# Adding the identity to W's blocks, starting the sums with ScalarE's copies, and building the images without rows of the first layer

## What is computed

```python
B_req = B[adapter_ids]; A_req = A[adapter_ids]
Bx = jnp.einsum('bni,bri->bnr', x, B_req)
out = jnp.einsum('bnr,bor->bno', Bx, A_req)            # layer 0, SCALING 1
...
base_out = jnp.einsum('bti,oi->bto', x, W) + b
lora_h = jnp.einsum('bti,bir->btr', x, A)
lora_out = jnp.einsum('btr,bro->bto', lora_h, Bm)
return base_out + lora_out * SCALING                   # layer 1, SCALING 2
...
x = x + _L0_cond_ref(x, L0_cond_A, L0_cond_B, itok_B_4_50)
x = x + _L1_cond_ref(x, itok_B_0_23, L1_cond_W, L1_cond_b, L1_cond_lora_As, L1_cond_lora_Bs)
```

## Time and profile before

| | before |
|---|---|
| median of 3 runs | 1411.78 us (1410.3 to 1412.83) |
| profiled execution | 1409.31 us |
| its span, first to last instruction | 1407.5 us |
| PE busy | 1373.3 us (98%) |
| DVE busy | 967.0 us (69%) |
| ACT busy | 484.7 us (34%) |
| POOL busy | 94.1 us (7%) |
| bytes moved | 320.98 MB, 228 GB/s over the span |
| granted TensorE clock, mean | 0.994 |

### The profile page before, as it was taken

The page is one execution under the profiler, slowest core; times in us unless marked ns, Lnnn a source line. Parts: engine busy times, 40 slices in busy tenths (PEclk is TensorE's granted clock), DMA queues, the critical chain, the costliest instruction groups (busy, mean ns, idle before and its releaser), DMA issues.

```text
span 1407.5 us, 16133 instructions
## 1 busy us (share of the span) xinstructions
PE 1373.3 (98%) x5992; PEld 1128.7 (80%) x5992; DVE 967.0 (69%) x1015; ACT 484.7 (34%) x491; POOL 94.1 (7%) x194
## 2 busy tenths in 40 slices
PE   5999989999999999999999999999999999999999
PEld 4787778888878888888888888888888888888887
DVE  5778777786768897666646676666655766666662
ACT  3444344323223333333323343333233334332331
POOL 3013210001000000000001000000101000000000
PEclk9999999999999999999999999999999999999999
DMA  9988863798999898466757334456856444457642
GB/s 348 317 291 292 282 233 131 258 376 300 317 355 336 302 303 291 166 220 233 240 198 241 128 120 156 169 187 214 276 199 228 141 137 135 154 171 249 197 152 83
DMA packets 106094, 320.98 MB, mean 228 GB/s; under 512 B 14240, under 2 KB 15392, under 8 KB 106016
## 3 DMA queue, kind: packets, MB, share of 16 engines
q1 hardware_dynamic: 99360, 307.35, 63.8%
q0 software_dynamic: 6656, 12.60, 2.8%
HBM read 264.31 MB, written 55.57 MB: 227 GB/s over the span
## 4 chain that ended last, share of the span: by engine, by line
PE 86%; DMA 6%; DVE 4%; issue 2%; SPq 1%; ACT 1%; POOLq 0%; POOL 0%; DVEq 0%; ACTq 0%
PE acc L546 26%; PE acc L547 26%; PE acc L548 26%; PE down_ps L516 2%; PE acc L530 2%; PE down_ps L517 2%; DMA bg_raw<-w_rows 1%; DMA w_two<-w 1%; DVE bg_lo L720 1%; DMA w_sums<-w_one 1%; DVE w_one L689 1%; DVE w_lo L693 1%; DMA bg_raw<-x 1%; PE image_ps L498 1%; DMA image<-a 1%
## 5 line engine op out<-in xcount | busy, mean ns | idle before, releaser
L546 PE MATMUL acc<-x_hi,w_hi 128*128 128x512 f32 x1792 | 704.5, 393 | 18.9 <-DVE x_lo L715 13.6
L547 PE MATMUL acc<-x_lo,w_hi 128*128 128x512 f32 x1792 | 701.4, 391 | 0.0
L548 PE MATMUL acc<-x_hi,w_lo 128*128 128x512 f32 x1792 | 700.9, 391 | 0.0
L583 ACT ACTIVATE w_hi<-w_one 128x1024 fp32r<-128x1024 f32 x224 | 237.4, 1060 | 679.1 <-PE acc L548 620.2
L546 PEld LDWEIGHTS acc<-x_hi,w_hi 128*128 128x128 f32 x1792 | 338.6, 189 | 92.8 <-issue 14.0
L547 PEld LDWEIGHTS acc<-x_lo,w_hi 128*128 128x128 f32 x1792 | 338.7, 189 | 71.8 <-issue 1.0
L548 PEld LDWEIGHTS acc<-x_hi,w_lo 128*128 128x128 f32 x1792 | 338.1, 189 | 71.4
L693 DVE TENSOR_TENSOR w_lo<-w_one,w_hi 128x1024 fp32r<-128x1024 f32 x224 | 273.7, 1222 | 110.1 <-ACT w_hi L583 110.1
L758 DVE SCALAR_TENSOR_TENSOR sums<-acc,bias_sb,sums 128x512 f32<-128x512 f32 x128 | 95.7, 748 | 43.6 <-PE acc L530 43.6
L715 DVE TENSOR_TENSOR x_lo<-x_stage,x_hi 128x1024 fp32r<-128x1024 f32 x80 | 96.1, 1222 | 43.0 <-ACT x_hi L602 42.8
L602 ACT ACTIVATE x_hi<-x_stage 128x1024 fp32r<-128x1024 f32 x80 | 83.4, 1056 | 103.9 <-DVE x_stage L709 82.2
(11 more groups left out here) (54 smaller groups left out, 628.6 us busy)
## 6 DMA issues: line engine op xcount, KB each, us to landing
w_one<-w SPq DMA_DIRECT2D x128, 512.0 KB, 5.6
w_one<-w_sums SPq DMA_DIRECT2D x96, 512.0 KB, 3.2
w_two<-w SPq DMA_DIRECT2D x64, 512.0 KB, 8.0
x_stage<-x SPq DMA_DIRECT2D x64, 512.0 KB, 4.6
out<-sums SPq DMA_DIRECT2D x128, 256.0 KB, 4.4
w_sums<-w_one SPq DMA_DIRECT2D x40, 512.0 KB, 5.3
resident<-x SPq DMA_DIRECT2D x32, 512.0 KB, 7.0
sums<-x SPq DMA_DIRECT2D x64, 256.0 KB, 4.9
```

Source lines behind the costliest of these rows:

```text
L546: pe.matmul(ps[:, :], w_hi[ws][:, c, :], hi, start=(c == 0), stop=False)
L547: pe.matmul(ps[:, :], w_hi[ws][:, c, :], lo, start=False, stop=False)
L548: mm = pe.matmul(ps[:, :], w_lo[ws][:, c, :], hi, start=False, stop=(c == H - 1))
L583: act.activation(w_hi[s % W_PARTS][:, :, :], w_one[s % W_ONES][:, :, :], ACT.Copy).then_inc(w_hi_ready, 1)
```

## The change

Instead of adding x when the banks are added, the identity (times -1, 1 or 2) is added to the diagonal part of W's blocks, so that the seven products give x (I + W^T). `make_w` does this in VectorE behind the sum, for 128 blocks. The tiles of `sums` now begin with ScalarE's copy of a bank (products 0, 1 and 4), VectorE's `add` has one addition where it had two in products 0 and 1, and none in product 4; `load_sum` is gone. Low-rank rows of layer 0 come into the image over TensorE (`wa` times the identity, 128 columns). The images' tile is now `b1_rows` itself; the closing product stands one step later at c = 6, and VectorE's copy one round later. Chunks of x (`z >= IMAGE`) are loaded a step earlier.

```diff
+W_IDENTITY = [-1.0, 2.0, 1.0, 1.0, -1.0, 1.0, 1.0]
+COPIED = [0, 1, 4]
...
-            image = sb("image", [P, T], F32, early)
...
+        image = b1_rows
...
             def keep_sum(s):
                 if keeps_sum(s):
-                    sp.wait_ge(w_summed, sums_before(s) + 1)
+                    sp.wait_ge(w_made, made_before(s) + 1)
...
                 for z in background(s + 2):
-                    load_bg(z)
-                if s + 2 < STEPS:
-                    load_sum(s + 2)
+                    if z < IMAGE:
+                        load_bg(z)
+                for z in background(s + 3):
+                    if z >= IMAGE:
+                        load_bg(z)
...
             def load_rows(j):
                 cols = slice(T * j, T * (j + 1))
                 if j:
-                    pool.wait_ge(image_done, j)
+                    keep_image(j - 1)
+                    pool.wait_ge(image_stored, DMA * j)
                 for n in range(NB):
                     pool.dma_start(b1_rows[R * n:R * (n + 1), :], adapter(1, n, b1).rearrange("u r d -> (u r) d")[:, cols])\
                         .then_inc(b1_rows_loaded, DMA)
-                if j:
-                    keep_image(j - 1)
-                    pool.wait_ge(image_stored, DMA * j)
-                for n in range(NB):
-                    pool.dma_start(image[R * n:R * (n + 1), :], adapter(0, n, a0).rearrange("u r d -> (u r) d")[:, cols])\
-                        .then_inc(a0_rows_loaded, DMA)
...
             pool.dma_start(ids_sb[:, 1, :], ids1).then_inc(ids_loaded, DMA)
+            pool.dma_start(identity_sb[:, :], identity).then_inc(identity_loaded, DMA)
...
+                        if c // BANKS == j:
+                            part = ps[:, P * (c % BANKS):P * (c % BANKS + 1)]
+                            pe.matmul(part, wa[0], identity_sb[:, :], start=False, stop=False)
+                            pe.matmul(part, wa[1], identity_sb[:, :], start=False, stop=False)
...
+            def end_image(j):
+                pe.wait_ge(across_ready, 1)
+                pe.wait_ge(b1_rows_loaded, NB * DMA * (j + 1))
+                pe.matmul(image_ps[j % 2][:, :], across[:, :], b1_rows[:, :],
+                          start=False, stop=True).then_inc(image_done, 1)
...
-                if i != 6:
-                    pe.wait_ge(first_added, 24 * g + 8 * (i - 3) + o + 1)
+                if i == 4:
+                    pe.wait_ge(copied, copied_before(s) + 1)
...
+                    if c == 6 and s - 1 in IMAGE_LAST:
+                        end_image(IMAGE_LAST[s - 1])
...
+            def copy(s):
...
+                if i == 1:
+                    act.wait_ge(bank_free, released_before(s) + 1)
+                else:
+                    act.wait_ge(step_done, s + 1)
...
+                act.activation(sums[1 if i == 1 else 2][:, o, :], acc[s % BANKS][:, :], ACT.Copy).then_inc(copied, 1)
...
+                    dve.wait_ge(w_summed, k + 1)
+                if s == 0:
+                    dve.wait_ge(identity_loaded, DMA)
+                dve.scalar_tensor_tensor(out=one[:, o, :], in0=f32(identity_sb[:, :]), scalar=W_IDENTITY[i],
+                                         in1=one[:, o, :], op0=ALU.mult, op1=ALU.add).then_inc(w_made, 1)
...
-                if s - 1 in IMAGE_LAST:
-                    j = IMAGE_LAST[s - 1]
+                if s - 2 in IMAGE_LAST:
+                    j = IMAGE_LAST[s - 2]
                     dve.wait_ge(image_done, j + 1)
-                    dve.wait_ge(a0_rows_loaded, NB * DMA * (j + 1))
-                    dve.tensor_tensor(image[:, :], image_ps[j % 2][:, :], image[:, :], ALU.add).then_inc(image_ready, 1)
+                    dve.tensor_copy(image[:, :], image_ps[j % 2][:, :]).then_inc(image_ready, 1)
```

More of the change, by code:

```diff
@@ L129, in has_sum, with is_made, made_before, copied_before @@
     return s >= 0 and i in SUMMED and g <= KEPT_IN[i]
+def is_made(s):
+    return s >= 0 and (has_sum(s) or where(s)[1] not in SUMMED)
+def made_before(s):
+    return sum(is_made(t) for t in range(s))
+def copied_before(s):
+    return sum(where(t)[1] in COPIED for t in range(s))
+def released_before(s):
+    return sum(where(t)[1] in RELEASED for t in range(s))
 def keeps_sum(s):
@@ L137, in sums_before @@
     return sum(has_sum(t) for t in range(s))
+SUM_STEPS = [s for s in range(STEPS) if has_sum(s)]
 def kept_in_slot(s):
@@ L164, in last_staged, with build @@
     return q
-def build(nc, x, ids0, ids1, a0, a0_down, b0, w, w_rows, bias, a1, b1, mask, w_sums, images, out):
+def build(nc, x, ids0, ids1, a0_down, b0, w, w_rows, bias, a1, b1, identity, mask, w_sums, images, out):
     with ExitStack() as ctx:
@@ L249, in build @@
         step_done = sem("step_done")
+        copied = sem("copied")
         first_added = sem("first_added")
         bank_free = sem("bank_free")
-        sum_loaded = [sem(f"sum_loaded{o}") for o in range(H)]
         out_stored = [sem(f"out_stored{o}") for o in range(H)]
@@ L380, in _ @@
             load_w(1)
-            load_sum(0)
-            load_resident(0, 0, 0)
             load_w(2)
-            load_sum(1)
-            load_resident(0, 0, 1)
+            for r in range(2):
+                load_resident(0, 0, r)
             for s in range(STEPS):
@@ L499, in multiply_chunk @@
                         pe.matmul(ps[:, :], wa[1], hi[:, u, :], start=False, stop=False)
+                        if c // BANKS == j:
+                            part = ps[:, P * (c % BANKS):P * (c % BANKS + 1)]
+                            pe.matmul(part, wa[0], identity_sb[:, :], start=False, stop=False)
+                            pe.matmul(part, wa[1], identity_sb[:, :], start=False, stop=False)
                         mm = pe.matmul(ps[:, :], wa[0], lo[:, u, :], start=False, stop=False)
                     mm.then_inc(bg_used, 1)
[L502 to L506, removed]
-                                  start=False, stop=True).then_inc(image_done, 1)
                     return
@@ L538, in step @@
                 if s >= BANKS:
-                    pe.wait_ge(bank_free, s - BANKS + 1)
+                    before = where(s - BANKS)[1]
+                    if before in (0, 1):
+                        pe.wait_ge(copied, copied_before(s - BANKS) + 1)
+                    elif before in RELEASED:
+                        pe.wait_ge(bank_free, released_before(s - BANKS) + 1)
                 pe.wait_ge(w_ready, s + 1)
@@ L602, in split_x @@
                 act.activation(x_hi[q % X_PARTS][:, :, :], x_source(p, r), ACT.Copy).then_inc(x_hi_ready, 1)
+            def copy(s):
+                g, i, o = where(s)
+                if i not in COPIED:
+                    return
+                if i == 1:
+                    act.wait_ge(bank_free, released_before(s) + 1)
+                else:
+                    act.wait_ge(step_done, s + 1)
+                stored = 4 * g + (-1, -2, None, None, 1)[i]
+                if stored > 0:
+                    act.wait_ge(out_stored[o], DMA * stored)
+                act.activation(sums[1 if i == 1 else 2][:, o, :], acc[s % BANKS][:, :], ACT.Copy).then_inc(copied, 1)
             def split_bg(z):
@@ L655, in _ @@
                     split_w(s + 1)
+                if s >= 1:
+                    copy(s - 1)
                 if s == 1:
@@ L858 @@
         "b1": laid(L1_cond_lora_Bs, (n1, R, D), (0, 1, 2)),
+        "identity": np.eye(P, dtype=np.float32),
         "mask": np.kron(np.eye(NB), np.full((R, R), SCALE1)).astype(np.float32),
```

74 lines of the change are left out of this document (34 added, 40 removed).

## The result

The changed kernel takes 1438.48 us (median of 4 runs, 1436.65 to 1441.7) against 1411.91 us before: 1.0192 times, 95% interval 1.017 to 1.0214, so 26.6 us slower. The forecast was 1436, range 1416 to 1453. The profiled execution spans 1435.3 us.

The account below looks back on a forecast made before the run. TensorE's product count was taken as the bound, so new TensorE stops decide: +22.4 + 6 + 3.7 - 4.3 - 1.6 + 0.8 - 0.5 + 1.5 - 3.5 = +24.5, giving 1434 profiled, 1436 us median; range 1416 to 1453.

Parts of the forecast that it names:

- stops of 9 to 33 us in all: The forecast's own case: TensorE waits for the next image's rows at three closing products; chance 82%.
- chains, 3 L: L is the time from VectorE's image copy to the landing of the eighth row load: 21.9 us, bounds 17.5 to 25.3.
- clock behind them: Low granted TensorE clock after each of the three image stops: 2.0 us each, +6 (3 to 8.4).
- small products: 32 TensorE products of 128 columns bring layer 0's rows into the images: 0.115 us each, +3.7 (1.8 to 7.3).
- start: First product 0.4 to 1.8 us late for the identity, then repaid by fewer loads and additions: -4.3 at step 5.
- stops under bg_lo, later pairs: Three TensorE stops of 0.6 us under bg_lo were to lose about 0.5 us together.
- ScalarE's copies: Bank copies of 0.57 us, hidden except in steps 35 and 37, where TensorE is delayed: +1.5 for both (0 to 3).
- stop at 418 us: TensorE's wait there for a chunk of x, now loaded a step earlier: -3.5 of 6.3 us with the clock.
- L - 15.2, L - 13.4 and L - 14.7: Predicted TensorE stops for images 0, 1 and 2, chain less work left meanwhile; together 3 L - 43.3, +22.4 us.
- the rival of the empty queues: Row loads land fast because nothing else loads while TensorE stands; under L = 15 no stops, 1410 us; chance 7%.
- the third rival: ScalarE's copies stop TensorE in all 32 steps of product 4, +32 to 1468 us; needs 1.4 us copies; chance 4%.
- reliefs in full: Images don't stop TensorE, and start and 418 us give their full 7 and 6 us: -7, 1405 us; chance 7%.

Follow-up runs that it names:

- second profile: The changed kernel run once more without any edit, with its own profile: 1438.16 us, ratio 1.0183 to the kernel before.
- experiment 9: 32 small identity products left out, on the changed kernel with images in their own tile, earlier identity, mixed chunk order and two copies moved: 1404.09 us, ratio 0.9949.
- experiment 5: Identity loaded first, over ScalarE's queue, on the changed kernel with images 0 to 2 in their own tile: 1413.42 us, ratio 1.002.
- experiment 8: 128 unused VectorE reads of 512 columns where additions were removed, on the changed kernel with images 0 to 2 in their own tile: 1416.67 us, ratio 1.0046.
- experiment 3: All x chunks loaded at their old place, two steps ahead instead of three, on the changed kernel: 1443.9 us, ratio 1.0221.
- Experiment 2: Only the images' part of the change, on the kernel before; sums, residual and chunk order as before: 1439.08 us, ratio 1.0211.
- experiment 1: Images 0 to 2 in a tile of their own (the space of down_raw), on the changed kernel: 1413.98 us, ratio 1.0019.
- experiment 4: Eight row-load addresses read once and kept in registers, on the changed kernel: 1430.17 us, ratio 1.0132.

## Why the prediction was right

The forecast of 1436 us was the case "stops of 9 to 33 us in all", and the measured 1438.48 is that case. Step by step:

| step of the sum | predicted | measured |
|---|---|---|
| chains, 3 L | 65.7 | 63.7 (23.4, 24.4, 15.9) |
| stops | +22.4 (6.7, 8.5, 7.2) | +20.0 (7.1, 10.4, 2.6) |
| clock behind them | +6 | about +5.7 |
| small products | +3.7 | +3.3 to +4.3 |
| start | -4.3 | -2.3, with image 0's 8 small products (+1.0) in it |
| stop at 130.7 us | -1.6 | gone; 0.7 at 110.1 is new |
| identity, with the `down` stop | +0.8 | -0.7 at `down`; +0.6 in the second profile |
| stops under bg_lo, later pairs | -0.5 | +0.9 |
| ScalarE's copies | +1.5 | +1.3 |
| stop at 418 us | -3.5 | -2.2; -3.9 in the second profile |
| stop at 223 us | not in the sum | +5.1; with `down` and the next step +4.1, in the second profile +3.9 |

The measured terms overlap and don't add up to the 27.8 us between the spans: with the small products counted once and 4.1 at 223 us and `down` together they come to about 29. The `x_lo` stop, which the sum held only inside the third chain, takes 1.1 off: 0.6 more of stop, 1.7 less of low clock.

- **The chain.** L - 15.2, L - 13.4 and L - 14.7 with the measured L give 8.2, 11.0 and 1.2 where the trace has 7.1, 10.4 and 2.6: the positions counted in products hold to 0.6 to 1.4 us. One L for all three was the weak part. The first two were 1.5 and 2.5 us over it, the third 6 below, which is the rival of the empty queues come true for one image of three. In part the landing was read from the wrong row: 4.1 us is that of `image<-a`, while the rows for which TensorE waits stood in the same view of the kernel before (95 to 180 us) as

```profile
b_rows<-b POOLq DMA_DIRECT2D x16, 32.0 KB, 5.6
```

  With it L is 23.4, and the last rows of the first two images landed in 5.4 and 5.8. The Trainium skill's fit (DMA: Bandwidth & Descriptors, SWDGE anatomy) gives an estimate of 2.6 us for the store and 2.1 for a row load; even in the third image the trace has 3.7 and 3.7, with 2.1 for the last row alone.
- **The clock.** The stretches behind the stops (last three numbers: granted clock, DMA share, GB/s):

```profile
125.00:129.00 4.00, 4.00 (x8) 2.48 (x9) 0.69 (x1) 0.63 (x1) 0.00 (x0) 0.50 0.65 255
...
185.50:188.50 3.00, 2.99 (x15) 2.51 (x16) 3.00 (x4) 0.60 (x1) 0.00 (x0) 1.00 0.86 240
199.60:205.00 5.40, 5.40 (x15) 4.00 (x16) 2.83 (x3) 1.06 (x1) 0.56 (x1) 0.68 0.13 49
```

  Behind the first, 4.29 us go by between 124.95 and 129.24 for what takes 2.2 at full clock (0.45 and 0.64 at the closing product, as at 88 us, and five at 0.227): 2.1 lost, where 2.0 was taken. Over the three it is 27.6 us with the stops, less 20.0 and less 1.9 that the closing products take anyway: 5.7. In the second profile the third stop has no such price (granted clock 1.00 from 200.8 to 206.0 us, behind 2.59 us).
- **The small products** cost what the 32 passes of the earlier trace rows said: 0.12 us each by the timeline, 0.10 to 0.13 by leaving them out (experiment 9).
- **The start** had the right cause with too large a size. VectorE's first block waits for the identity:

```profile
9.82 0.29 DVE L738 SCALAR_TENSOR_TENSOR w_one<-identity_sb,w_one 128x128 f32<-128x128 f32 x1 [2.20 <-DMA identity_sb<-identity]
```

  The first product came 2.4 us late, above the 0.4 to 1.8 allowed, and it was paid back as predicted (experiment 5). The relief at step 5 is 2.3 us, 3.3 without the small products, for 4.3 taken. I counted on fewer loads and on VectorE's 1.2 us a step, and experiment 8 shows that the second is worth nothing there.
- **The x_lo stop in step 16** was to grow from 2.2 to 2.8 and is 2.84. That the clock would stay at 1.00 behind it (above), where it had been 0.54 before, I did not see; the 1.7 us of the earlier trace rows were saved by it. It is part of the -1.2 up to step 17, and it is luck of the run: in experiment 3 the clock behind the same stop is 0.50.
- **ScalarE's copies** stop TensorE exactly twice, at the two steps that were named; in the timeline of ScalarE at the first of them

```profile
322.69 1.06 ACT L607 ACTIVATE w_hi<-w_one 128x1024 fp32r<-128x1024 f32 x1 [2.75 <-DVE w_one L738]
323.66 0.58 ACT L640 ACTIVATE sums<-acc 128x512 f32<-128x512 f32 x1
```

  each by 0.6 us. A copy takes 0.58 us where 0.57 was assumed, so the third rival is out: it needed 1.4.
- **The bg_lo stops** were given the wrong sign. I took them to shrink by the additions that are gone. They grew from 0.57, 0.57 and 0.53 to 0.85 us each (478.8, 527.1 and 575.5 us). Experiment 2, which has neither the identity in W's blocks nor fewer additions, has 0.57, 0.56 and 0.52: the growth comes from that part of the change, and 0.29 us is what one identity operation takes. The group of `w_lo` fits:

```profile
L743 DVE TENSOR_TENSOR w_lo<-w_one,w_hi 128x1024 fp32r<-128x1024 f32 x224 | 274.2, 1224 | 208.4 <-ACT w_hi L607 208.1
```

  VectorE waits 208.4 us ahead of `w_lo`, against 110.1 before: work taken away ahead of a wait makes the wait longer and the end no earlier, while the identity's 0.29 us stands on the path to `w_hi`. But the additions would not be free beside it: with their time given back (experiment 8) the first two of the three stops are 1.52 and 1.34 us.
- **The stop at 223 us** is the step that was missing. The move of the chunk loads was costed at 418 us, where it helps, and not at the first pair, where the earlier load waits for its buffer with the loads of W behind it.

That the sum came out so near is in part luck: this +5.1 stood against 2.4 too much in the stops, and in the stops two chains that were too short stood against one that was too long. Of the rivals, "reliefs in full" had -7 without the stops; experiment 1 measured +2.7 with the small products' 3.7 in it. That is -1.0 for everything else, and the change has hardly a gain to set against its stops.

## What to carry to other kernels

When two tiles are made one, write down the whole chain that the new reuse puts between "last reader" and "refilled" (copy, store, landing, address reads, loads, landing) and count in products of the bounding engine when it is needed: the stops here followed to 1.4 us or less once the chain's length was known, and a second tile in space that was free at the time took away 23.9 of 26.6 us. Time taken off an engine counts only where no wait stands between that work and its consumer: ask which wait will grow by it. And a load that is moved earlier in an in-order list is to be checked at every place where its buffer may be taken, not only where it helps.

## What the runs showed of the hardware, not expected

- Eight row loads of 32 KB on GpSimd's queue took 10.0 us together whether issued over 4.0 or 8.0 us (experiment 4, third image); the last alone, with little else in the queues, landed in 2.1 us.
- A stop doesn't always lower the clock, and not the same in every execution: behind 2.84 us at 185.5 us the granted clock is 1.00, in experiment 3 behind the same stop 0.50, and behind 2.24 us at the same place before it is 0.54. Behind 2.56 us at 199.5 us it is 0.68, and behind 2.59 us there in the second profile 1.00. What decides isn't shown.
- The closing product of an image (f32, not split) is dear at the low clock: from its start to that of the second product behind it 2.26 us at 124.95, against 1.09 at 88.15.
